# Sinkhorn temporaries of the last stage: from SBUF to a PSUM bank, with one PSUM buffer for the branch product

## The reference, cut to what matters

```python
Z = (x_norm @ W_res.T + H_res_base) / tau          # 4 x 4 logits for each token
def step(carry, _):                                # 50 times
    u = -logsumexp(Z + v[..., None, :], axis=-1)
    v = -logsumexp(Z + u[..., :, None], axis=-2)
H_res = exp(Z + u[..., :, None] + v[..., None, :])
H_res = (1.0 - g) * I + g * H_res
x_pre = einsum('btnc,btn->btc', x_streams, H_pre)
y = x_pre @ W_branch                               # the branch product
x_mixed = einsum('btij,btjc->btic', H_res, x_streams)
out = x + x_mixed + einsum('btc,btn->btnc', y, H_post)
```

## Time and profile before

| | us |
|---|---|
| median of three runs | 1073.83 |
| the profiled execution, its own time | 1075.11 |
| its span, first to last instruction | 1073.3 |
| the Sinkhorn part, from the first instruction of VectorE in `stage_e` to the first of the tail | 86.92 |
| the tail, from there to the end of the span | 30.13 |

### The profile page before, as it was taken

The page is one execution under the profiler, slowest core; times in us unless marked ns, Lnnn a source line. Parts: engine busy times, 40 slices in busy tenths (PEclk is TensorE's granted clock), DMA queues, the critical chain, the costliest instruction groups (busy, mean ns, idle before and its releaser), DMA issues. The chain is left out here.

```text
span 1073.3 us, 20195 instructions
## 1 busy us (share of the span) xinstructions
PE 1032.0 (96%) x7174; PEld 780.3 (73%) x7174; DVE 874.6 (81%) x1881; ACT 663.5 (62%) x1127; POOL 93.8 (9%) x85
## 2 busy tenths in 40 slices
PE   8999999999999999999999999999999999956978
PEld 7888888777777777777777777776888887534637
DVE  5764544799999999999999999975764895879998
ACT  5332320498989899898998989862331114635826
POOL 0221011200000000000000000000002112400000
PEclk9999999999999999999999999999999999987989
DMA  8548779841123232123323212158315000000003
GB/s 328 182 166 297 258 262 280 314 121 37 45 75 73 68 73 70 37 45 73 73 68 73 66 39 48 50 202 276 118 59 171 0 0 1 1 1 1 1 1 156
DMA packets 55568, 112.95 MB, mean 105 GB/s; under 512 B 7724, under 2 KB 21164, under 8 KB 55388
## 3 DMA queue, kind: packets, MB, share of 16 engines
q1 hardware_dynamic: 55452, 112.26, 33.6%
q0 software_dynamic: 64, 0.00, 0.0%
HBM read 83.99 MB, written 27.26 MB: 104 GB/s over the span
## 5 line engine op out<-in xcount | busy, mean ns | idle before, releaser
L898 DVE CUSTOM_DVE_ANT_0 XS<-b_psS,b_mbias 128x1024 f32<-128x1024 f32 x256 | 311.1, 1215 | 0.9 <-PE b_psS L778 0.7
L853 ACT ACTIVATE XS<-XS,b_mins 128x1024 f32<-128x1024 f32 x256 | 295.5, 1154 | 10.1 <-DVE b_mins L898 9.5
L811 PEld LDWEIGHTS b_psT<-ident,XS 128*128 128x128 f32 x2048 | 229.9, 140 | 65.8 <-issue 47.6
L811 PE MATMUL b_psT<-ident,XS 128*128 128x128 f32 x2048 | 271.9, 276 | 1.6 <-ACT b_PT L861 1.6
L907 DVE COPY b_PT<-b_psT 128x512 f32<-128x512 f32 x256 | 176.9, 691 | 26.8 <-PE b_psT L811 25.1
L861 ACT COPY b_PT<-b_psT 128x512 f32<-128x512 f32 x256 | 149.7, 585 | 38.8 <-PE b_psT L811 30.8
L778 PE MATMUL b_psS<-XTh 128*128 128x512 f32 x512 | 155.9, 422 | 0.7 <-PEq L115 0.6
L792 PE MATMUL b_psO<-b_PT,XTh 128*32 128x256 f32 x1984 | 132.8, 385 | 0.0
L778 PEld LDWEIGHTS b_psS<-XTh 128*128 128x128 f32 x512 | 85.1, 189 | 18.5 <-DVE b_mins L898 7.7
L792 PEld LDWEIGHTS b_psO<-b_PT,XTh 128*32 128x32 f32 x1984 | 51.8, 109 | 42.1 <-issue 20.8
L415 ACT ACTIVATE a_oh<-a_psM 128x512 fp32r<-128x512 f32 x24 | 14.2, 597 | 80.1 <-PE a_psM L335 53.5
(11 more groups left out here) (270 smaller groups left out, 1613.9 us busy)
## 6 DMA issues: line engine op xcount, KB each, us to landing
XS<-in_ctx SPq DMA_DIRECT2D x16, 512.0 KB, 5.6
XTh<-QHd SPq DMA_DIRECT2D x32, 256.0 KB, 4.5
XTh<-QLd SPq DMA_DIRECT2D x32, 256.0 KB, 5.0
XS<-in_ctx_turned SPq DMA_DIRECT2D x8, 512.0 KB, 10.9
XS<-in_x SPq DMA_DIRECT2D x8, 512.0 KB, 11.9
a_wst<-in_L_xattn_w_q SPq DMA_DIRECT2D x8, 512.0 KB, 5.5
a_xn<-in_ctx_turned SPq DMA_DIRECT2D x8, 512.0 KB, 4.1
QHd<-a_oh SPq DMA_DIRECT2D x16, 256.0 KB, 5.4
```

Of the source, the lines that this page charges most:

```text
L811: last_t = pe.transpose(psT[:, kt, :], Pr[:, k % PR, kt * P:(kt + 1) * P], ident[:])
L853: act.activation(Pr[:, k % PR, :], Sc[:, k % 4, :], ACT.Exp, bias=mins[:, k % 4:k % 4 + 1], scale=-1.0, accum_out=sums[:, u, j:j + 1]).the ...
L898: dve.tensor_tensor_reduce(out=Sc[:, k % 4, :], in0=psS[:, k % 2, :], in1=mbias[:, qt, :], scale=1.0, scalar=3.4e38, op0=ALU.add, op1=ALU.min,
```

## The change

`T`, `zx`, `ra` and `cb` are no longer tiles in SBUF but parts of bank 1 of `psY2` in PSUM. So `psY`, which had a buffer in each bank, has one, in bank 0, and `branch_product(t)` waits until `post_scale(t - 1)` is done (it was `t - 2`). `Z2`, a new tile in SBUF, takes the difference that ScalarE's exponentials read (it was `T`). The last two products write `Z` in SBUF. `M`, `MT`, `Z`, `zc` and `E0` stay in SBUF. The load of tile 7's row goes into bank 1, so TensorE issues it only after `sink`, just ahead of that tile's own products.

```diff
-        zx = sb("e_zx", [P, NT, STREAMS])
-        T = sb("e_T", [P, NT, STREAMS, STREAMS])
-        ra = sb("e_ra", [P, NT, STREAMS])
-        cb = sb("e_cb", [P, NT, STREAMS])
+        Z2 = sb("e_Z2", [P, NT, STREAMS, STREAMS])
...
-        psY = [psY2[:, u, 0:CH] for u in range(2)]
+        psY = psY2[:, 0, 0:CH]
+        NF = NT * NR
+        NV = NT * STREAMS
+        T = psY2[:, 1, 0:NF].rearrange("p (t i j) -> p t i j", t=NT, i=STREAMS)
+        zx, ra, cb = (psY2[:, 1, NF + u * NV:NF + (u + 1) * NV].rearrange("p (t i) -> p t i", t=NT) for u in range(3))
...
             def branch_product(t):
                 pe.wait_ge(pre_kept, t + 1)
-                if t >= 2:
-                    pe.wait_ge(post_scaled, t - 1)
+                if t:
+                    pe.wait_ge(post_scaled, t)
                 for k in range(CHT):
-                    last = pe.matmul(psY[t % 2], xpT[:, t % 2, k, :], wb[:, k, :], start=(k == 0), stop=(k == CHT - 1))
+                    last = pe.matmul(psY, xpT[:, t % 2, k, :], wb[:, k, :], start=(k == 0), stop=(k == CHT - 1))
...
-            for t in range(NT):
+            def rows_in(t):
                 pe.matmul(psZ[t][:, 0:pe_rows(t) * CH], ident[:], XR[:, t, (STREAMS - pe_rows(t)) * CH:],
                           start=True, stop=False)
+            for t in range(NT - 1):
+                rows_in(t)
             done = 0
             for t in range(NT):
                 rows = pe_rows(t)
+                if t == NT - 1:
+                    pe.wait_ge(sink, 1)
+                    rows_in(t)
...
-            act.activation(MT[:], T[:].rearrange("p t i j -> p t j i"), ACT.Exp, bias=lift[:, 0:1]).then_inc(exps, 1)
-            act.activation(M[:], T[:], ACT.Exp, bias=lift[:, 0:1]).then_inc(exps, 1)
+            act.activation(MT[:], Z2[:].rearrange("p t i j -> p t j i"), ACT.Exp, bias=lift[:, 0:1]).then_inc(exps, 1)
+            act.activation(M[:], Z2[:], ACT.Exp, bias=lift[:, 0:1]).then_inc(exps, 1)
...
-            times(n, 3, ra, T, M)
-            times(n + CHAINS, 2, cb, T, T)
+            times(n, 3, ra, Z, M)
+            times(n + CHAINS, 2, cb, Z, Z)
...
-            Tf = T[:].rearrange("p t i j -> p t (i j)")
+            Tf = Z[:].rearrange("p t i j -> p t (i j)")
```

More of the change, by code:

```diff
@@ L2060, in post_scale @@
                 for n in range(STREAMS):
-                    last = act.activation(yp[:, t % 2, n * CH:(n + 1) * CH], psY[t % 2], ACT.Copy,
+                    last = act.activation(yp[:, t % 2, n * CH:(n + 1) * CH], psY, ACT.Copy,
                                           scale=hp[:, t, STREAMS + n:STREAMS + n + 1])
@@ L2114, in _ @@
             Zl = LG[:, :, 0:NR].rearrange("p t (i j) -> p t i j", i=STREAMS)
-            dve.tensor_reduce(zx[:], Zl, AX.X, ALU.max).then_inc(lg, 1)
+            dve.tensor_reduce(zx, Zl, AX.X, ALU.max).then_inc(lg, 1)
             dve.wait_ge(lg, 1)
-            dve.tensor_tensor(Z[:], Zl, over(zx[:], STREAMS), ALU.subtract).then_inc(lg, 1)
+            dve.tensor_tensor(Z[:], Zl, over(zx, STREAMS), ALU.subtract).then_inc(lg, 1)
             dve.wait_ge(lg, 2)
@@ L2121, in _ @@
             dve.wait_ge(lg, 3)
-            dve.tensor_tensor(T[:], Z[:], zc[:].unsqueeze(2).to_broadcast([P, NT, STREAMS, STREAMS]), ALU.subtract
+            dve.tensor_tensor(Z2[:], Z[:], zc[:].unsqueeze(2).to_broadcast([P, NT, STREAMS, STREAMS]), ALU.subtract
                               ).then_inc(lg, 1)
             dve.wait_ge(exps, 1)
-            dve.tensor_reduce(zx[:], E0[:], AX.X, ALU.add).then_inc(lg, 1)
+            dve.tensor_reduce(zx, E0[:], AX.X, ALU.add).then_inc(lg, 1)
             dve.wait_ge(lg, 5)
-            dve.reciprocal(ra[:], zx[:]).then_inc(lg, 1)
+            dve.reciprocal(ra, zx).then_inc(lg, 1)
             dve.tensor_reduce(mx[:], LG[:, :, NR:NL].rearrange("p t (g n) -> p t g n", g=2), AX.X, ALU.max
```

## The result

The changed kernel takes 1076.55 us against 1073.90 before (medians of 20 runs each); the ratio is 1.0026, with a 95% interval of 1.0018 to 1.0035. By the interval it is 1.9 to 3.8 us slower. The middle lies within the 0.3% that the forecast took for no measurable change, the upper end doesn't; and the whole interval is on the slower side of nothing.

The account below looks back on a forecast made before the run. VectorE's queue in the Sinkhorn iterations was taken to bind; 0.8 us for PSUM reads plus 0.4 us for the late row load made +1.2 us, 1075.0 on the median; overall range 1064 to 1085, the forecast's own 1072 to 1077.

Parts of the forecast that it names:

- its two terms: In the last stage: 0.8 us for sums and reciprocals reading PSUM, 0.4 us for tile 7's row load in the tail.
- the prediction's signs: Sinkhorn half step (six VectorE instructions) of 0.81 to 0.82 us, sums 210 to 215 ns, store's end 0.4 us later.
- VectorE's queue binds, the data does not: Sinkhorn iterations: VectorE's instruction occupancies set the 0.81 us half step; data is ready 7 to 19 ns earlier.
- Writing to PSUM: 594 Sinkhorn instructions: taken as 0, bounded by -41 ns (gain 0) and +41 ns (+8.4 us).
- The part on the slack: Sinkhorn half step: a slower write costs only beyond slacks of 19, 7 and 12 ns; a faster one gains nothing.
- Reading from PSUM: Sinkhorn iterations: 0 for 198 products, +2 ns for each of 396 sums and reciprocals, 0.8 us; ends -2.4 and +2.0 us.
- Rival C: Sinkhorn iterations: a small PSUM operand costs VectorE a fixed time, 16.2 or 24.4 us, giving 1090.4 to 1098.6; chance 0.08.
- The tail: Tile 7's row load moves from TensorE's idle time to mid-tail: two records, 0.43 us, all showing at the end.
- The single buffer: Branch product on TensorE: its new wait for `post_scaled` is always met when reached, so 0.
- Rival A: Sinkhorn iterations: VectorE's queue gets shorter with source and target in PSUM, 1068.3 or 1064.6 us; chance 0.30.
- Rival B: Sinkhorn iterations: results take longer into PSUM, beyond 7 ns; 1075.4 us at 15 ns, 1082.6 at 41; chance 0.22.
- Rival D: TensorE stalls on the single buffer's wait or the late row; less than a microsecond or two; chance 0.02.

## Why the prediction was right

The forecast was no measurable change, +1.2 us, with slower more likely than its two terms might suggest; measured were +2.65 us (1.9 to 3.8), at the upper edge of the forecast's own range of 1072 to 1077. By the prediction's signs the picture is less clean than the number: the half step was to be 0.81 to 0.82 us and the sums 210 to 215 ns long, and they are 0.83 and 225. That is inside the 0.78 to 0.84 beyond which the forecast was to be wrong, but the mechanism cost more than the terms that it was given.

**VectorE's queue binds, the data does not: held.** It binds in the changed kernel as well. A result's end and its reader's start lie at least 40 ns apart there, over the bare 34 to 35, and only the pairs of instructions that read PSUM alone took longer when a temporary was moved. With one group, where the data binds, the same change costs 30 ns in place of 21.

**Writing to PSUM: held, with a size that was left open, and partly by luck.** The bounds were -41 and +41 ns with 0 taken. It is +8 ns on a row. The part on the slack said that it costs only beyond 7 ns; the smallest slack is 8 to 9 ns in the trace's nanoseconds (a step of 43 over the bare 34 to 35), and with `zx`, or `ra` and `cb`, in PSUM the step is 36 and no spacing behind the write grew. The margin was narrow, 1 or 2 ns, and nothing in the prediction had put the write on this side of it.

**Reading from PSUM: the term that was mis-sized.** I took +2 ns for the 396 sums and reciprocals, 0.8 us, between +5 from the reduce of 192 columns and -6 from the copies. The nearest row, the reduce, was nearly right, and the copies pulled the value down. Measured are 6 to 7 ns each, above even the upper end of +5 (2.0 us). They were compared with another operation, the statistics, and a difference of 6 ns between two operations says nothing on their sources. By starts it is +26 ns a half step on two sums and two reciprocals, 2.6 us over 99, and -5 ns on the two products, whose 0 was so also a little off: +21 ns a half step, 2.1 us. With the 0.4 of the tail that is 2.5 us, and 2.2 by the two windows; the runs' interval holds both.

The rule of the Trainium skill (page "VectorE: DVE Perf Modes", section on the TRN2 errata: 58 cycles from SBUF, 120 from PSUM) has the right sign and the wrong size for the sums and reciprocals: 5 to 7 ns are about 5 to 7 cycles at its 0.96 GHz, not 62. For the products it has the wrong sign, since they took no longer. Rival C, a large fixed cost of a small PSUM operand, is excluded with it: it wanted a half step of 1.06 us.

**The tail: held.** 0.43 us was worked out from 0.217 us a record, and the load takes 0.43 us on the chain. Moving it into idle time gives all of it back.

**The single buffer: held.** `post_sum` ahead of `branch_product` already had the same wait; the branch keeps its 6.08 us a tile.

**Rival A** (a shorter queue with both sides in PSUM) fell: sums with source and target there take 135 and 132, more than with the source in SBUF. ScalarE's advantage from PSUM did not carry over. **Rival B** had its write, 8 ns, but not its price: the slack just held it. Its sign was a half step over 0.83 us with steps of 0.03 between a result and its reader; the half step is there (0.833), the steps are not (0.040 and more), and the runs put the cost on the sources. **Rival D**, a stall of TensorE, fell with the single buffer and the tail.

## What to carry to other kernels

Where two groups alternate on an engine, ask whether the queue or the data sets the pace: compare each end-to-start step with the bare semaphore step, and take costs from the starts, since two rows that are 7 and 9 ns longer can cost 7 and 0. In a chain like this one, small temporaries of VectorE belong in SBUF; the one operand that was not dearer in PSUM is the second source of a product. If a move frees a bank late, put the load that waits for the bank where its engine is idle anyway, not just ahead of its use.

## What the runs showed of the hardware that was not expected

- On VectorE, with 64 and fewer columns: a PSUM source costs a sum or a reciprocal 5 to 7 ns of occupancy (mean of the pair), and a product with the other source in SBUF costs 1 to 4 ns less than with both there. A PSUM target adds 8 to 9 ns to the row and none to the occupancy; with four groups, where a row overlaps the next by 77 ns with the target in SBUF and by 88 to 90 with the target in PSUM, it adds 11 to 13.
- With `zx` in PSUM the first reciprocal of a pair took 172 ns and the second 126, so the whole 11 ns fell on the first; with everything in PSUM it was 168 and 133. Why it falls so is open.
- TensorE's clock after idle time, as seen and not isolated: no run changed the idle time alone. In the kernels with one group TensorE stood idle for 2.40 us (SBUF) and 4.32 us (PSUM) before the tail, against 1.42 in the kernel before and 1.10 in the changed one. The granted clock over the first 4 us of the tail was 0.65 (a mix of the two levels) and 0.50 (all at 1.2 GHz), against 1.00 (all at 2.4 GHz) in the changed kernel, and the tail took 31.81 and 32.94 us in place of 30.13 and 30.54. The first stretch of the tail with one group, SBUF, then PSUM, then the changed kernel (the clock is the number after GpSimd's):

```profile
1060.89:1065.00 4.11, 3.66 (x10) 3.04 (x11) 4.11 (x11) 4.11 (x15) 0.00 (x0) 0.65 0.02 6
```

```profile
1066.06:1070.20 4.14, 3.69 (x9) 2.97 (x10) 4.14 (x11) 4.14 (x15) 0.00 (x0) 0.50 0.03 6
```

```profile
1042.66:1046.80 4.14, 3.68 (x17) 3.27 (x18) 4.14 (x11) 4.14 (x15) 0.00 (x0) 1.00 0.03 6
```

TensorE issued 9 to 10 products there in place of 17. With four groups it was the same: 3.14 and 4.43 us idle, 0.58 and 0.50 over the first 4.1 us, and tails of 31.61 and 32.97 us. So the time of these kernels (1094.5 and 1100.8 us with one group, 1099.35 and 1106.69 with four, one run each) is only in part VectorE's: of the 6.3 us between the two with one group the Sinkhorn part has 2.85 and the tail 1.1.
